# One of three fields of the sorted edges placed by GpSimd instead of VectorE

## The chip, the cores and the metric

The kernel runs on 1 core of one Trainium2 chip. The metric is the device time of one execution in microseconds (us), lower is better; a version's time is the median of its runs.

## What is computed

The reference is four message-passing layers over one graph: 3125 nodes with 128 features, 103125 directed edges. Each layer normalizes the node features, gathers them along the edges, and sums or softmax-averages messages at the edges' targets:

```python
edge_index = jnp.stack([src, dst])
h = jnp.maximum(_layernorm(x, axis=-1), 0.0)
x = x + _L0_gnn_ref(h, edge_index, edge_attr_32, edge_type_2, edge_weight, ...)
h = jnp.maximum(_layernorm(x, axis=-1), 0.0)
x = x + _L1_gnn_ref(h, L1_gnn_W1, L1_gnn_w2, src, dst)
h = jnp.maximum(_layernorm(x, axis=-1), 0.0)
x = x + _L2_gnn_ref(h, edge_index, edge_attr_2, ...)
h = jnp.maximum(_layernorm(x, axis=-1), 0.0)
x = x + _L3_gnn_ref(h, edge_index, edge_type_16, ...)
```

The change is in none of the layers but in what prepares the last three of them: the edges are sorted by the block of 128 nodes in which their source lies, so that a layer can work on dense blocks.

## The kernel before, in words

After layer 0 the kernel sorts the edges once. The nodes form NB = 25 blocks of 128. All edges whose target lies in block b make bucket b; a bucket is read as a window of 128 x 36 edges (EPP = 36 edges in each of 128 partitions) and is spread over KT = 50 tiles of 128 edges, two for each source block. An edge has three fields to carry along: a packed word (edge type, source and target within their blocks) and two attributes.

The five engines run the sort as a pipeline over the buckets, each with its own loop in program order, and semaphores between them. Per bucket:

- **SyncE** (`sp_sort`) loads the window `edge_in` into a ring of RING_E = 4 buffers and stores the finished bucket's rows.
- **VectorE, classes** (`dve_classes`, L2850, L2853) marks which of the 25 source blocks each edge belongs to, and counts.
- **VectorE, route** (`dve_route`, L2858 to L2878) gives each edge a slot: a scan and a reduce (L2860 to L2862), then tile number `tile_i` and position `pos_i`. L2874 writes `minus_pos`, which ScalarE waits for. L2875 writes the mask `in_tile` (128 x 36 x 50: edge is in tile k), and L2878 multiplies it by the three fields into `routed_v` (128 x 36 x 3 x 50), the multiply that is changed.
- **ScalarE** (`act_sort`) turns the positions into one-hot columns `hot_pos`: 36 instructions of L2957, then L2960 over all of them.
- **TensorE** (`pe_sort`, L2994) multiplies, for each of the 36 edges of a partition, one-hot position by routed fields and adds up in PSUM. In the profile that is 72 matmuls a bucket, of 128x150.
- **VectorE, unpack** (`dve_unpack`, L2884 to L2903) takes the sums out of PSUM and splits the packed word by many operations on 128x50 integers, then the attributes into bf16 parts.
- **GpSimd** does nothing in this loop.

`hot_pos`, `routed_v` and `minus_pos` have two buffers, `edge_in` four; `in_tile` has one. VectorE's order is fixed by the loop of `dve_sort`:

```python
for n in range(NB + 2):
    if n < NB:
        dve_classes(e, own, n)
    if 0 <= n - 1 < NB:
        dve_route(e, own, n - 1)
    if n >= 2:
        dve_unpack(e, own, n - 2)
```

So after the multiply of bucket b comes the unpacking of bucket b-1, which waits for TensorE's sums of that bucket (`packed_pe`), then the classes of b+2 and the route of b+1. In the profile the tensors show by the arena they lie in: `in_tile`, `edge_in`, `member`, `rank`, `tile_i` in arena_b, `routed_v`, `unpack_i` in arena_a, `hot_pos` in arena_c. Later, in layers 1 to 3, GpSimd builds one-hot masks (L3119, L3411, L3129) and clears buffers (L3123) while VectorE works on other parts of the same layers.

Of the kernel before, what the change touches and what calls it, by code (L numbers as in the profile page):

```python
# [21 lines left out]
NB = -(-N // P)  # L22
# [60 lines left out]
def turns(k, ring):  # L83

    return k // ring + 1
# [218 lines left out]
class BucketSignals:  # L304


    def __init__(self, g):
        spare = iter(g.of_layer0() + g.of_runs())

        def pair():  # L310
            return [next(spare), next(spare)]


        self.own = next(spare)
        self.consts = next(spare)
        self.d_list = next(spare)
        self.listed = next(spare)
        self.d_table = next(spare)
        self.d_start = next(spare)
        self.start = next(spare)  # L320
        self.d_keys = g.d_begin_keys
        self.d_window = pair() + pair()
        self.tot_dve = next(spare)
        self.pre_pe = next(spare)
        self.pre_used = next(spare)
        self.routed = next(spare)
        self.weighed = next(spare)
        self.spread = next(spare)
        self.away = next(spare)
        self.packed_pe = next(spare)  # L330
        self.fields = next(spare)
        self.turned_pe = next(spare)
        self.rows_act = next(spare)
        self.d_rows = pair()
        self.flag = next(spare)

        self.d_logits = next(spare)
        self.spread_lo = next(spare)
        self.hot = next(spare)
        self.counted_pe = next(spare)  # L340
        self.counted_act = next(spare)
        self.maxed = next(spare)
        self.diag = next(spare)
        self.negmax_pe = next(spare)
        self.exps = next(spare)
        self.weights = next(spare)
        self.mean_pe = next(spare)
        self.mean_used = next(spare)

        self.d_small = next(spare)  # L350
        self.split_act = next(spare)
        self.split_dve = next(spare)
        self.wc_set = next(spare)
        self.d_wc = next(spare)
        self.d_unit = pair() + [self.d_table, self.d_logits]
        self.attr_zero = next(spare)
        self.row_hot = next(spare)
        self.h_pe = next(spare)
        self.squared = next(spare)
        self.terms_set = next(spare)  # L360
        self.summed = next(spare)

        self.d_counted = self.d_rows
        self.d_pair_count = self.d_window
        self.low = self.routed
        self.low3 = self.weighed
        self.col_hot_pool = self.spread
        self.col_hot3_pool = self.away
        self.drawn_pe = self.pre_pe
        self.drawn = self.tot_dve  # L370
        self.scaled = next(spare)
        self.relu = next(spare)
        self.col_hot = next(spare)
        self.added_pe = next(spare)
        self.block_dve = next(spare)
        self.extra_pe = next(spare)
        self.extra_dve = next(spare)

        self.types_set = next(spare)
        self.d_types = next(spare)  # L380
        self.d_unit3 = pair() + [self.d_start]
        self.d_chunk = self.d_list
        self.typed = self.consts
        self.types_zero = self.flag
        self.row_hot3 = next(spare)
        self.h3_pe = next(spare)
        self.relu3 = next(spare)
        self.col_hot3 = next(spare)
        self.added3_pe = next(spare)
        self.block3_dve = next(spare)  # L390


def program(nc, a, out):
    ctx = ExitStack()
    with ctx:
# [2367 lines left out]
        def sp_sort(e):  # L2763
            e.wait_ge(g.phase_ended, 4)
            for signal in g.of_layer0():
                cleared = e.sem_clear(signal)
            cleared.then_inc(g.phase_begun, 1)
            e.wait_ge(sig.listed, 1)
            sp_load_tiled(e, sig.d_list, raw_tiled[:, 0], a["src"], 1)
            sp_load_tiled(e, sig.d_list, raw_tiled[:, 1], a["dst"], 1)  # L2770
            sp_load_tiled(e, sig.d_list, raw_tiled[:, 2], a["edge_type_16"], 1)
            sp_load_tiled(e, sig.d_list, raw_attr, a["edge_attr_2"].rearrange("e k -> (e k)"), 2)
            e.dma_start(lasts, row_bc(first_last[1, :], NB)).then_inc(sig.d_start, 16)
            e.wait_ge(sig.start, 2)
            e.dma_start(start_row.rearrange("(b o) -> b o", o=1), begin_i[1], allow_slow_non_contiguous=True).then_inc(sig.d_start, 16)
            e.wait_ge(sig.d_start, 32)
            e.dma_start(begin_row_i, start_row.unsqueeze(0)).then_inc(sig.d_start, 16)
            e.wait_ge(sig.listed, 2)
            e.dma_start(edge_table.rearrange("(c p f) w -> p c (f w)", c=TC, p=P), edges.rearrange("p (c f) w -> p c (f w)", c=TC)).then_inc(sig.d_table, 16)
            e.wait_ge(sig.d_start, 48)  # L2780
            e.wait_ge(sig.d_table, 16)
            for n in range(NB + 3):
                for j in (0, 1, 2) if n == 0 else (n + 2,):
                    if j < NB:
                        s = j % RING_E
                        if j >= RING_E:
                            e.wait_ge(sig.weighed, j - RING_E + 1)
                        first = e.value_load(begin_row_i[0:1, j:j + 1], min_val=0, max_val=E)
                        e.dma_start(edge_in[s], edge_table[bass.ds(first, WINDOW), :].rearrange("(p j) w -> p j w", p=P)).then_inc(sig.d_window[s], 16)
                if n >= 3:  # L2790
                    sp_store_bucket(e, n - 3)
            e.wait_ge(sig.flag, 1)
# [62 lines left out]
        def dve_route(e, own, b):  # L2855
            s = b % 2
            e.wait_ge(sig.pre_pe, b + 1)
            own.step(e.tensor_tensor(member[s][:, :, 0], bank[s][:, 0:NB], class_base, ALU.add))  # L2858
            flat = lambda v: v.rearrange("p k j -> p (k j)")
            own.step(e.tensor_tensor_scan(flat(rank), flat(restart), flat(member[s]), 0.0, ALU.mult, ALU.add))  # L2860
            own.step(e.tensor_tensor(rank[:, :, 1:], rank[:, :, 1:], member[s][:, :, 1:], ALU.mult))
            own.mark(e.tensor_reduce(slot_f, rank[:, :, 1:].rearrange("p k j -> p j k"), AX, ALU.add))  # L2862
            if b < NB - 1:

                own.step(e.tensor_scalar(over_f, rank[:, b, 1:], (2.0 * b + 3) * P, (KT - 2 * b - 3.0) * P, ALU.is_ge, ALU.mult))
                own.step(e.tensor_tensor(slot_i, slot_f, over_f, ALU.add))
            else:
                own.settle()
                own.step(e.tensor_copy(slot_i, slot_f))
            own.mark(e.tensor_scalar(tile_i, slot_i, 7, None, ALU.arith_shift_right))  # L2870
            own.step(e.tensor_scalar(pos_i, slot_i, P - 1, None, ALU.bitwise_and))
            if b >= 2:
                e.wait_ge(sig.packed_pe, b - 1)
            e.tensor_scalar(minus_pos[s], pos_i, -1.0, None, ALU.mult).then_inc(sig.routed, 1)  # L2874
            own.step(e.tensor_tensor(in_tile, bc(tile_i, 2, KT), bc(tile_row, 1, EPP), ALU.is_equal))  # L2875
            if b == 0:
                e.wait_ge(sig.squared, 1)
            e.tensor_tensor(routed_v[s], bc(in_tile, 2, 3), bc(edge_in[b % RING_E][:, :, 1:4], 3, KT), ALU.mult).then_inc(sig.weighed, 1)  # L2878

        def dve_unpack(e, own, b):  # L2880
            s = b % 2
# [54 lines left out]
        def pool_sort(e):  # L2936
# [3 lines left out]
            e.iota(tile_row, [[1, KT]], base=1, channel_multiplier=0, allow_small_or_imprecise_dtypes=True).then_inc(sig.consts, 1)  # L2940
            e.wait_ge(sig.start, 1)
            pool_gather(e, first_of, dst_keys, begin_i[0], sig.d_keys)
            e.wait_ge(sig.flag, 1)

        def act_sort(e):
# [30 lines left out]
        def pe_sort(e):  # L2976
            pause(e)
            for n in range(NB + 2):
# [7 lines left out]
                if 0 <= n - 1 < NB:  # L2986
                    b = n - 1
                    s = b % 2
                    e.wait_ge(sig.spread, b + 1)
                    e.wait_ge(sig.weighed, b + 1)  # L2990
                    if b >= 2:
                        e.wait_ge(sig.fields, b - 1)
                    for j in range(EPP):
# [18 lines left out]
        def sp_buckets(e):  # L3012
# [43 lines left out]
                sp_unit3(e, u)  # L3056
            e.wait_ge(g.nodes_ready, 8)
            sp_feature_rows(e, ("L3_gnn_msg_b", "L3_gnn_upd_b", "L3_gnn_ln_g", "L3_gnn_ln_b"))
            e.wait_ge(sig.types_set, 1)
            for i in range(3):  # L3060
                e.dma_start(E48[NT16 * i:NT16 * (i + 1), :], em_parts[:, i, :]).then_inc(sig.d_types, 16)
            for u in range(RING_U, 2 * NB):
# [4 lines left out]

        def sp_wc(e):

            e.wait_ge(sig.wc_set, 1)  # L3070
            for row, (i, part) in enumerate(((0, 0), (0, 1), (0, 2), (1, 0), (1, 1), (1, 2), (0, 0), (0, 1), (1, 0), (1, 1), (0, 0), (1, 0))):
                e.dma_start(Wc12[row:row + 1, :], wc_parts[i:i + 1, part, :]).then_inc(sig.d_wc, 16)

# [781 lines left out]
```

## Time and profile before

| | before |
|---|---|
| median of 3 runs | 4701.85 us (4698.02 to 4704.81) |
| the profiled execution, its own time | 4679.63 us |
| its span in the profile | 4677.9 us |
| VectorE busy | 3316.0 us (71%) |
| TensorE busy, matmuls | 3381.6 us (72%) |
| ScalarE busy | 2085.2 us (45%) |
| GpSimd busy | 1899.9 us (41%) |

The profiled execution is 22 us shorter than the median of the runs, so a sum made on its rows is a difference, to be added to either time. "Busy" counts an instruction from its start to its end in the record; an instruction that has been issued but is held up inside its engine counts as busy too. Consecutive instructions of an engine overlap by up to some 0.1 us in the record. The sort's loop over buckets lies from 2081 to 2574 us of the span. Outside it the change touches only two waits of SyncE, by their counts.

### The profile page before, as it was taken

The page shows a single profiled execution, that of the slowest core. Times are in us where ns is not written, and L with a number is a line of the kernel's source. Part 1 is how long each engine was busy: PE and PEld are TensorE (multiplying, and loading weights), DVE is VectorE, ACT ScalarE, POOL GpSimd, SP SyncE. Part 2 cuts the span into 40 slices and gives each one's busy share as a digit, 9 for nine tenths or more (in the row PEclk, how much of TensorE's full clock was granted, in tenths as well). Part 3 has the DMA queues.
Part 4 walks back from the last instruction along what each step waited for, and adds up shares of the span by engine and source line. Part 5 has one row for each costly group of instructions (what it writes and reads, how often), then busy time and mean ns, then how long its engine had stood idle before and what let it go on. Part 6 is the DMA issues. An engine that isn't in the chain of part 4 may idle for free.

```text
span 4677.9 us, 86004 instructions
## 1 busy us (share of the span) xinstructions
PE 3381.6 (72%) x31039; PEld 2815.7 (60%) x31039; DVE 3316.0 (71%) x6623; ACT 2085.2 (45%) x6143; POOL 1899.9 (41%) x2178
## 2 busy tenths in 40 slices
PE   1477777777777776326666467885789999969996
PEld 1255544454555554216666367784489999859995
DVE  5476666665666665459998688786766666679997
ACT  2344444444545553228787356673022222224443
POOL 0355566665666664100000130000045555538884
PEclk7677777776777776667777688997899999979998
DMA  4655555564555553010000121102344444313332
GB/s 108 187 156 155 154 160 154 155 153 142 166 159 167 158 167 103 16 38 8 12 12 9 56 79 60 43 38 90 117 122 125 126 126 126 107 53 127 128 129 70
DMA packets 368019, 498.45 MB, mean 107 GB/s; under 512 B 76530, under 2 KB 307636, under 8 KB 367453
## 3 DMA queue, kind: packets, MB, share of 16 engines
q1 hardware_dynamic: 313437, 328.51, 23.1%
q0 software_dynamic: 54144, 164.25, 12.6%
q8 instruction: 256, 4.19, 0.4%
q14 instruction: 182, 1.49, 0.1%
HBM read 381.76 MB, written 110.84 MB: 105 GB/s over the span
## 4 chain that ended last, share of the span: by engine, by line
PE 40%; DVE 22%; ACT 14%; issue 10%; another core or an unknown queue 5%; POOL 4%; DMA 3%; SPq 2%; ACTq 0%; DVEq 0%; POOLq 0%
PE psum L3691 4%; PE psum L3707 3%; PE psum L3642 3%; PE psum L3640 3%; PE psum L2490 3%; POOL arena_a L1172 3%; ACT arena_a L1366 3%; PE psum L2994 3%; ACT arena_c L2957 3%; PE psum L3607 2%; DVE arena_a L3187 2%; PE psum L3666 2%; PE psum L2425 2%; PE psum L3689 2%
## 5 line engine op out<-in xcount | busy, mean ns | idle before, releaser
L1172 POOL DMA_INDIRECT arena_a<-src_table,src_tix x808 | 820.8, 1016 | 430.1 <-issue 385.2
L3411 POOL TENSOR_SCALAR node_hot<-arena_c 128x128 fp32r<-128x128 f32 x575 | 368.7, 652 | 901.8 <-DVE arena_c L3299 568.6
L3429 DVE SCALAR_TENSOR_TENSOR msg_parts<-psum,msg_parts 128x512 fp32r<-128x512 f32 (+2 forms) x644 | 425.3, 660 | 259.9 <-ACT msg_parts L3578 227.8
L3129 POOL TENSOR_SCALAR node_hot_dst<-arena_c 128x128 fp32r<-128x128 f32 x587 | 383.9, 671 | 122.4 <-DVE arena_c L3533 67.9
L3578 ACT ACTIVATE msg_parts<-psum 128x512 fp32r<-128x512 f32 (+2 forms) x325 | 186.4, 574 | 520.4 <-PE psum L3642 520.4
L2994 PE MATMUL psum<-arena_a,arena_c 128*128 128x150 f32 x1800 | 289.4, 331 | 173.3 <-ACT arena_c L2960 173.3
L3640 PE MATMUL psum<-arena_c,arena_a 128*128 128x128 bf16 x3675 | 406.4, 220 | 0.0
L3642 PE MATMUL psum<-arena_c,arena_a 128*128 128x128 bf16 x3675 | 406.4, 220 | 0.0
L2994 PEld LDWEIGHTS psum<-arena_a,arena_c 128*128 128x128 f32 x1800 | 283.8, 225 | 176.4 <-ACT arena_c L2960 176.4
L1366 ACT ACTIVATE arena_a<-arena_a 128x128 f32<-128x128 f32 x808 | 238.5, 300 | 338.6 <-issue 259.2
L2433 PE MATMUL psum<-win_parts,pick_w 128*128 128x256 f32 x1616 | 381.4, 387 | 0.1
L2433 PEld LDWEIGHTS psum<-win_parts,pick_w 128*128 128x128 f32 x1616 | 274.5, 231 | 149.8 <-issue 148.8
L2408 PE MATMUL psum<-arena_b,win_w 3*128 3x512 bf16 x202 | 93.1, 461 | 357.3 <-ACT pick_w L1383 299.5
L3119 POOL TENSOR_SCALAR arena_a<-arena_a,arena_c 128x2500 bf16<-128x2500 bf16 x8 | 63.5, 7937 | 705.5 <-DMA arena_a<-bucket_lists 705.5
L1352 ACT ACTIVATE arena_c<-psum 128x272 f32<-128x272 f32 x404 | 161.0, 399 | 413.1 <-remote 323.2
L3638 PE MATMUL psum<-src_tix,arena_a 128*128 128x128 bf16 x1225 | 272.4, 222 | 70.9 <-DVE arena_a L3315 37.2
L2425 PE MATMUL psum<-weights,arena_c 128*128 128x512 f32 x404 | 318.8, 882 | 0.0
L1853 DVE TENSOR_TENSOR arena_a<-arena_a,psum 128x512 f32<-128x512 f32 x202 | 138.7, 687 | 251.9 <-remote 184.1
L1210 POOL TENSOR_TENSOR arena_c<-arena_c,weights 128x8 f32<-128x8 f32 x101 | 171.4, 1697 | 357.1 <-ACT arena_a L1366 354.2
L3691 PE MATMUL psum<-arena_c,arena_a 128*128 128x128 bf16 x3675 | 308.9, 219 | 0.0
L2957 ACT ACTIVATE arena_c<-arena_c,arena_b 128x128 f32<-128x128 f32 x900 | 265.8, 387 | 90.1 <-DVE arena_b L2874 90.1
L3593 ACT ACTIVATE msg_parts<-psum 128x512 fp32r<-128x512 f32 (+1 forms) x319 | 185.4, 581 | 260.4 <-PE psum L3691 260.4
(581 smaller groups left out, 10177.8 us busy)
## 6 DMA issues: line engine op xcount, KB each, us to landing
y_rows<-arena_c SPq DMA_DIRECT2D x101, 576.0 KB
arena_a<-bucket_rows SPq DMA_DIRECT2D x150, 384.0 KB
arena_a<-bucket_rows SPq DMA_DIRECT2D x50, 448.0 KB
arena_a<-bucket_lists SPq DMA_DIRECT2D x25, 896.0 KB
pair_counts<-arena_c SPq DMA_DIRECT2D x25, 800.0 KB
arena_a<-bucket_lists SPq DMA_DIRECT2D x25, 704.0 KB
arena_a<-src_table,src_tix POOLq DMA_INDIRECT x808
arena_c<-edge_attr SPq DMA_DIRECT2D x101, 128.0 KB
```

Source lines behind the costliest of these rows:

```text
L1172: e.indirect_dma_start(out_, None, table, bass.IndirectOffsetOnAxis(ap=idx, axis=0)).then_inc(sem, 16)
L1366: sq = e.activation(GS[r][:, t, 2 * D:3 * D], GS[r][:, t, 2 * D:3 * D], ACT.Square, accum_out=d2[:, t:t + 1])
L2425: e.matmul(bank[0][:, :], eat[k % RING_EA][:, hf, :], Wt4[:, :], start=True, stop=True).then_inc(g.addend_pe, 1)
L2433: rows = e.matmul(picked[:, t, :], pick_w[s][:, 4 * hf + t, :], win_parts[s][:, part, :], start=(part == 0), stop=(part == 1))
L2957: away = e.activation(hot_pos[s][:, j, :], iota_row, ACT.Abs, bias=minus_pos[s][:, j:j + 1])
L2994: put = e.matmul(bank[2 + s][:, 0:3 * KT], hot_pos[s][:, j, :], routed_v[s][:, j, :, :].rearrange("p f k -> p (f k)"), start=(j == 0), sto ...
L3129: return e.tensor_scalar(node_hot3[at % RING_H][:, i, :], iota_row, dst_lo[:, b, t:t + 1], None, ALU.is_equal)
L3411: return e.tensor_scalar(node_hot[at % RING_M][:, i, :], iota_row, src_lo[:, b, 2 * k + j:2 * k + j + 1], None, ALU.is_equal)
L3429: e.scalar_tensor_tensor(out=to[:, 1, 0:nt, :], in0=bank[at % 4][:, 0:nt * P].rearrange("p (t f) -> p t f", f=P), scalar=0.0, in1=to[:, 0, ...
L3640: e.matmul(to, row_hot[0][s][:, c_], A3[:, part, sb_ * D:(sb_ + 1) * D], start=False, stop=False)
L3642: put = e.matmul(to, row_hot[1][s][:, c_], B3[:, part, b * D:(b + 1) * D], start=False, stop=(part == 2))
L3691: put = e.matmul(to, src_rows3[s][:, c_], A3[:, part, k * D:(k + 1) * D], start=False, stop=(part == 2))
```

## The change

The multiply that places the fields is split. VectorE still makes the mask and multiplies it by two of the fields (the packed word and the first attribute), 128 x 3600 elements in place of 128 x 5400. GpSimd gets a loop of its own over the 25 buckets in `pool_sort`: for each it waits for the window, for the mask and for the free buffer of `routed_v`, and multiplies the mask by the second attribute, 128 x 1800 elements. Both read the same mask, and both wait for the same count of the new semaphore `tiled`, which the mask's instruction raises. VectorE writes the next mask only when GpSimd has done with this one (`weighed_pool`, b), TensorE starts its matmuls only when both parts are there, and SyncE refills a window's buffer only when both have read it. `tiled` and `weighed_pool` share semaphores with `types_set` and `wc_set`, whose waits now start from NB = 25.

```diff
--- before.py
+++ after.py
@@ -347,6 +347,7 @@
         self.mean_pe = next(spare)
         self.mean_used = next(spare)
 
+        self.types_set = next(spare)
         self.d_small = next(spare)
         self.split_act = next(spare)
         self.split_dve = next(spare)
@@ -360,6 +361,8 @@
         self.terms_set = next(spare)
         self.summed = next(spare)
 
+        self.tiled = self.types_set
+        self.weighed_pool = self.wc_set
         self.d_counted = self.d_rows
         self.d_pair_count = self.d_window
         self.low = self.routed
@@ -376,7 +379,6 @@
         self.extra_pe = next(spare)
         self.extra_dve = next(spare)
 
-        self.types_set = next(spare)
         self.d_types = next(spare)
         self.d_unit3 = pair() + [self.d_start]
         self.d_chunk = self.d_list
@@ -2785,6 +2787,7 @@
                         s = j % RING_E
                         if j >= RING_E:
                             e.wait_ge(sig.weighed, j - RING_E + 1)
+                            e.wait_ge(sig.weighed_pool, j - RING_E + 1)
                         first = e.value_load(begin_row_i[0:1, j:j + 1], min_val=0, max_val=E)
                         e.dma_start(edge_in[s], edge_table[bass.ds(first, WINDOW), :].rearrange("(p j) w -> p j w", p=P)).then_inc(sig.d_window[s], 16)
                 if n >= 3:
@@ -2872,10 +2875,13 @@
             if b >= 2:
                 e.wait_ge(sig.packed_pe, b - 1)
             e.tensor_scalar(minus_pos[s], pos_i, -1.0, None, ALU.mult).then_inc(sig.routed, 1)
-            own.step(e.tensor_tensor(in_tile, bc(tile_i, 2, KT), bc(tile_row, 1, EPP), ALU.is_equal))
+            if b:
+                e.wait_ge(sig.weighed_pool, b)
+            e.tensor_tensor(in_tile, bc(tile_i, 2, KT), bc(tile_row, 1, EPP), ALU.is_equal).then_inc(sig.tiled, 1)
             if b == 0:
                 e.wait_ge(sig.squared, 1)
-            e.tensor_tensor(routed_v[s], bc(in_tile, 2, 3), bc(edge_in[b % RING_E][:, :, 1:4], 3, KT), ALU.mult).then_inc(sig.weighed, 1)
+            e.wait_ge(sig.tiled, b + 1)
+            e.tensor_tensor(routed_v[s][:, :, 0:2, :], bc(in_tile, 2, 2), bc(edge_in[b % RING_E][:, :, 1:3], 3, KT), ALU.mult).then_inc(sig.weighed, 1)
 
         def dve_unpack(e, own, b):
             s = b % 2
@@ -2940,6 +2946,14 @@
             e.iota(tile_row, [[1, KT]], base=1, channel_multiplier=0, allow_small_or_imprecise_dtypes=True).then_inc(sig.consts, 1)
             e.wait_ge(sig.start, 1)
             pool_gather(e, first_of, dst_keys, begin_i[0], sig.d_keys)
+
+            e.wait_ge(sig.squared, 1)
+            for b in range(NB):
+                e.wait_ge(sig.d_window[b % RING_E], 16 * turns(b, RING_E))
+                e.wait_ge(sig.tiled, b + 1)
+                if b >= 2:
+                    e.wait_ge(sig.packed_pe, b - 1)
+                e.tensor_tensor(routed_v[b % 2][:, :, 2, :], in_tile, bc(edge_in[b % RING_E][:, :, 3], 2, KT), ALU.mult).then_inc(sig.weighed_pool, 1)
             e.wait_ge(sig.flag, 1)
 
         def act_sort(e):
@@ -2988,6 +3002,7 @@
                     s = b % 2
                     e.wait_ge(sig.spread, b + 1)
                     e.wait_ge(sig.weighed, b + 1)
+                    e.wait_ge(sig.weighed_pool, b + 1)
                     if b >= 2:
                         e.wait_ge(sig.fields, b - 1)
                     for j in range(EPP):
@@ -3056,7 +3071,7 @@
                 sp_unit3(e, u)
             e.wait_ge(g.nodes_ready, 8)
             sp_feature_rows(e, ("L3_gnn_msg_b", "L3_gnn_upd_b", "L3_gnn_ln_g", "L3_gnn_ln_b"))
-            e.wait_ge(sig.types_set, 1)
+            e.wait_ge(sig.types_set, NB + 1)
             for i in range(3):
                 e.dma_start(E48[NT16 * i:NT16 * (i + 1), :], em_parts[:, i, :]).then_inc(sig.d_types, 16)
             for u in range(RING_U, 2 * NB):
@@ -3067,7 +3082,7 @@
 
         def sp_wc(e):
 
-            e.wait_ge(sig.wc_set, 1)
+            e.wait_ge(sig.wc_set, NB + 1)
             for row, (i, part) in enumerate(((0, 0), (0, 1), (0, 2), (1, 0), (1, 1), (1, 2), (0, 0), (0, 1), (1, 0), (1, 1), (0, 0), (1, 0))):
                 e.dma_start(Wc12[row:row + 1, :], wc_parts[i:i + 1, part, :]).then_inc(sig.d_wc, 16)
 
```

## Rows read from the trace of the kernel before

**Rows 1.** Chain that ended last, two buckets: start us, us, engine, tile, line, count

```profile
2149.34 10.64 ACT arena_c L2957 x36
2160.00 4.05 ACT arena_c L2960
...
2164.10 12.50 PE psum L2994 x72
2176.62 0.22 DVE arena_a L2884
...
2187.77 7.42 ACT arena_c L2957 x25
```

**Rows 2.** Timeline of VectorE, one bucket: start us, us, engine, line, op, out<-in

```profile
2130.37 0.18 DVE L2874 TENSOR_SCALAR arena_b<-arena_b 128x36 f32<-128x36 int32 x1
2130.47 2.03 DVE L2875 TENSOR_TENSOR arena_b<-arena_b,arena_a 128x1800 f32<-128x1800 int32 x1
2132.53 5.78 DVE L2878 TENSOR_TENSOR arena_a<-arena_b 128x5400 f32<-128x5400 f32 x1
2138.23 0.20 DVE L2884 CAST arena_a<-psum 128x50 int32<-128x50 f32 x1
2138.47 0.19 DVE L2885 TENSOR_SCALAR arena_a<-arena_a 128x50 int32<-128x50 int32 x1
...
2140.29 0.26 DVE L2903 TENSOR_TENSOR weights<-arena_a,weights 128x100 bf16<-128x100 f32 x1
2140.47 1.77 DVE L2850 TENSOR_TENSOR arena_b<-arena_b,arena_c 128x900 f32<-128x900 f32 x1
...
2149.12 0.18 DVE L2874 TENSOR_SCALAR arena_b<-arena_b 128x36 f32<-128x36 int32 x1
```

**Rows 3.** The line L2874 by its source: durations in ns min/median/max, first and last start

```profile
L2874 DVE TENSOR_SCALAR arena_b<-arena_b x25: 182/183/185, 2092.8 to 2543.8; 128x36 f32<-128x36 int32 x25
```

**Rows 4.** Busy time from the first L2874 to the last, by engine

```profile
2092.80:2543.80 451.00, 287.31 (x1862) 280.41 (x1863) 435.38 (x632) 367.85 (x956) 0.00 (x0) 0.77 0.05 10
```

**Rows 5.** Timeline of TensorE, one odd and one even bucket; in brackets the idle time before

```profile
2315.90 11.69 PE L2994 MATMUL psum<-arena_a,arena_c 128*128 128x150 f32 x72 [7.13 <-ACT arena_c L2960]
2334.64 10.88 PE L2994 MATMUL psum<-arena_a,arena_c 128*128 128x150 f32 x72 [6.18 <-ACT arena_c L2960]
```

**Rows 6.** Timeline of GpSimd, then of VectorE, around one L3119 in layer 1

```profile
2801.08 7.39 POOL L3119 TENSOR_SCALAR arena_a<-arena_a,arena_c 128x2500 bf16<-128x2500 bf16 x1 [20.82 <-DMA arena_a<-bucket_lists]
...
2801.41 0.68 DVE L3180 SCALAR_TENSOR_TENSOR arena_c<-arena_c 128x512 f32<-128x512 f32 x1
2802.01 6.23 DVE L3187 CUSTOM_DVE_ANT_0 arena_a<-arena_b,arena_a 128x512 f32<-128x512 f32 x1
...
2809.41 0.69 DVE L3187 CUSTOM_DVE_ANT_0 arena_a<-arena_b,arena_a 128x512 f32<-128x512 f32 x1
```

**Rows 7.** Timeline of VectorE, then of GpSimd, around the clearing L3123

```profile
4101.72 0.47 DVE L3411 TENSOR_SCALAR node_hot<-arena_c 128x128 fp32r<-128x128 f32 x2
...
4104.10 2.26 DVE L3411 TENSOR_SCALAR node_hot<-arena_c 128x128 fp32r<-128x128 f32 x2
...
4103.13 6.25 POOL L3123 MEMSET arena_a<- 128x3584 bf16 x2 [0.47 <-PE psum L3642]
```

**Rows 8.** Timeline of VectorE and of GpSimd, then GpSimd's line L3129 by its source

```profile
4303.84 1.15 DVE L3489 TENSOR_SCALAR arena_a<-arena_a,node_id 128x3584 bf16<-128x3584 bf16 x1
...
4304.23 1.22 POOL L3129 TENSOR_SCALAR node_hot_dst<-arena_c 128x128 fp32r<-128x128 f32 x1 [1.68 <-PE psum L3707]
...
L3129 POOL TENSOR_SCALAR node_hot_dst<-arena_c x587: 596/603/1443, 4180.3 to 4617.4; 128x128 fp32r<-128x128 f32 x196
```

**Rows 9.** Integer and float operations of VectorE by their source, as in rows 3

```profile
L2825 DVE TENSOR_SCALAR arena_c<-arena_a x1: 607/607/607, 2061.2 to 2061.2; 128x896 int32<-128x896 int32 x1
...
L2853 DVE TENSOR_REDUCE arena_b<-arena_b x25: 1090/1092/1093, 2083.2 to 2520.9; 128x25 f32<-128x900 f32 x25
```

**Rows 10.** GpSimd's clearing line by form: count, busy us, mean ns

```profile
L3123 POOL MEMSET arena_a<- 128x3584 bf16 x2 | 6.3, 3158 | 0.5 <-PE psum L3642 0.5
```

## The prediction

> **What bounds the kernel now.** I read the page first: the loop of the sort is 490 us of a span of 4678, and GpSimd idles in it. Then the chain of waits, to see which engine ends last there. It goes round: ScalarE from 2149.34, 10.64 + 4.05 us, then TensorE, 12.50 us, then VectorE from L2884 until the next L2874, then ScalarE again at 2187.77 [rows 1]. That round serves one bucket, and two rounds are under way at a time (odd and even buckets), so it takes 38.43 us for two buckets, 19.2 for one. Then VectorE's timeline over one bucket: from L2874 to L2874 it is 2149.12 - 2130.37 = 18.75 us without a gap [rows 2]. So two limits lie almost on each other: VectorE's own work of 18.75 a bucket, and the round of 18.7 to 19.2. All 25 buckets confirm it: first to last L2874 is 2543.8 - 2092.8 = 451.0 us for 24 steps, 18.79 each [rows 3], with VectorE busy for 435.4 us of it and GpSimd for none [rows 4]. The round varies with TensorE's part: 11.69 for an odd bucket, 10.88 for the even one behind it [rows 5].
>
> All times below count from T, the end of a bucket's L2874 (2130.55 in rows 2).
>
> **The change, part by part.**
>
> *VectorE's multiply gets shorter.* L2875 and L2878 have 1800 and 5400 elements and take 2.03 and 5.78 us [rows 2]: 3.75 us for 3600 elements, 1.04 ns each. With 3600 elements the multiply takes 5.78 - 1.88 = 3.90 us. It starts at T+1.98 and ends at T+5.88, where it ended at T+7.76. That alone gives little, since the round does not contain the multiply: ScalarE has started at T, and TensorE waits for ScalarE until T+14.8, long after the fields are there. VectorE would only wait for TensorE instead of working: its step would be 16.87 us, the round's 18.75. Even buckets, held up now by VectorE's order, could follow TensorE's shorter time [rows 5]: mean of 11.69 and 10.88 in place of 11.69 is 0.4 us per two buckets, at most 5 us in all.
>
> *GpSimd's multiply is added, and it shares something with VectorE.* Both multiplies start on the same count. What happens when the two engines meet is in layer 1 [rows 6]: while L3119 runs on GpSimd, VectorE's L3187 takes 6.23 us, and 0.69 us when alone. It was held for 5.54 us. GpSimd's instruction itself had begun 0.93 us before it got its way, at a boundary between two instructions of VectorE, and ended at 2808.47, 0.92 us after VectorE was let go (2808.24 - 0.69 = 2807.55). All eight L3119 have such a partner. So one excludes the other for whole instructions. By the Trainium skill ("SBUF — State Buffer", section "Who interferes with whom"), a VectorE instruction with two SBUF inputs, or one in a two-port mode, and a GpSimd instruction that reads SBUF block each other completely, the one that starts first going first; by that rule the trace agrees, with 6.23 against 0.69 us.
>
> *Which of the two goes first?* VectorE starts L2878 0.03 us after the mask [rows 2]; GpSimd has waits in front of it and needed up to 0.93 us from its start [rows 6]. I take VectorE first. GpSimd then gets in at T+5.88.
>
> *How long does it hold VectorE?* No row has this multiply. The nearest is L3119, a long GpSimd instruction that reads and writes a tile: 5.54 us for 2500 elements is 2.22 ns each, 3.99 us for 1800, and 0.92 us from there to its end. Bounds: below, the clearing, which reads nothing, with 3.16 us for 3584 elements [rows 10], 0.88 ns each, 1.6 us for 1800; above, the 128-element mask with 0.60 us [rows 8], 4.7 ns each, 8.5 us. By the skill's "GPSIMD Engine Reference", section "Performance versus the Vector engine", a two-input operation on 2048 fp32 elements takes 4497 ns, 3.95 us for 1800 if scaled (an estimate); with a hold of 3.6 the sum below would be +31 us instead.
>
> *What is held?* Behind the multiply stands the unpacking of the bucket before: L2884 reads PSUM, and from L2885 on come small operations on integers in SBUF, one input each. Do these wait too? Two rows say so. Two L3411 of VectorE, one input each, take 2.26 us during the clearing on GpSimd and 0.47 together before it [rows 7]; they end at 4106.36, so they were let go at 4105.9, about 0.3 us before the first of the two clearings ends (4103.13 + 3.16 [rows 10], less the overlap of the two). And GpSimd's L3129 takes 1.22 us during L3489 and 0.60 otherwise [rows 8]. The integer operations of the sort are of that fast kind: L2825 takes 0.607 us for 896 elements, where a reduce of 900 takes 1.09 [rows 9]. So L2885 waits for GpSimd, until somewhere between the end of its reads (3.99) and 0.3 before its end (3.99 + 0.92 - 0.3 = 4.6). I take 4.3.
>
> *The sum.* GpSimd holds from T+5.88 to T+10.18. From L2885 (2138.47) to the next T (2149.30) VectorE needs 10.83 us [rows 2]. The new step is 5.88 + 4.3 + 10.83 = 21.0 us against 18.79. The round is no longer the limit: TensorE's sums are there at 26.8 - 21.0 = T+5.8. The first and the last of the 24 steps lack a part: the first has no unpacking, about 18.6 (the blocked instruction is L2850, let go with the reads), the last has no classes (1.77 and 1.09 us), about 18.1. Sum: 22 x 21.0 + 18.6 + 18.1 = 498.7 us, against 451.0: **47.7 us more**. TensorE's wait for GpSimd's part is hidden: GpSimd ends at T+5.88+4.91 = T+10.8, TensorE starts at T+14.8. If GpSimd needed 4 us more, that cover would be gone. VectorE's next mask waits for GpSimd until T+10.8 and comes at T+21: hidden. SyncE's refill waits for a bucket three back: hidden. The profiled execution would go from 4679.6 to 4727.3; the median of the runs, 22 us higher, from 4701.85 to **4749.5**.
>
> **The rivals.**
>
> 1. *The small operations pass.* Then GpSimd's 3.99 us fall into VectorE's own idle time. VectorE waits for TensorE until T+8.0 anyway, then unpacks; the first operation with two SBUF inputs is L2903, 2.06 us later, at T+10.1, and GpSimd has read all by T+9.9. The step stays at the round: between 18.6 and 18.8, from 4697 to 4702, no slower. For it: 50 elements are few, and no row shows an operation that short being held. Against: rows 7 and 8. The same result comes if GpSimd is quicker than I think: the loss is gone when the hold is below 18.79 - 5.88 - 10.83 = 2.1 us, near the lower bound. Chance 0.19, 0.04 of it for a gain over 9 us.
> 2. *GpSimd goes first.* Then L2878 waits 4.0 us, ends at T+10.2, and L2884 to T follows with 11.07: a step of 21.2, 52 us more, 4754. For it: both wait for the same count. Against: the waits in front of GpSimd and its late start [rows 6]. Chance 0.10.
> 3. *GpSimd is slow.* With 8.5 us the hold makes a step of 25.2, about 150 us more, 4850, and TensorE begins to wait for it too. It speaks for it that short instructions cost that rate; against, that L3119 does not. Chance 0.05.
>
> The forecast has the rest, 0.66. That the change does less than it says cannot be: GpSimd has 25 new instructions and VectorE's multiply has a third less.
>
> **How the numbers follow.** A measurement of this kernel can tell about 0.2%, 9.4 us, from no change. The forecast's own range: a hold of 3.0 us gives +18 us, 4.9 gives +61, 5.4 gives +73. I give 4716 to 4775, which leaves out rival 1 and rival 3, and takes in rival 2. Faster by over 0.2%: 0.04. Within: 0.15 (rival 1). Slower: 0.81.
>
> **What would show it.** Right: one small operation behind L2884 recorded with some 4 us, in nearly every bucket; VectorE's multiply at 3.9 us; GpSimd's multiply recorded longer than its work (it waits 3.9 us for VectorE), some 8 us; a step of 21 us; no wait of L2884 for TensorE. Wrong in the kind: all small operations at 0.18 to 0.19 us and VectorE idle for 2 us before L2884, with the step at 18.7. Rival 2 would show a multiply of VectorE of 8 us and GpSimd's one of 5. The size is wrong if GpSimd's hold is not near 4.3 us.

## The result, and the profile after

| | before | changed |
|---|---|---|
| median of 5 runs | 4698.02 us (4693.24 to 4704.81) | 4717.76 us (4711.72 to 4722.67) |
| ratio | | 1.0045, 95% interval 1.0032 to 1.0058 |
| span of the profiled execution | 4677.9 us | 4718.2 us |

By the medians the change costs 19.7 us, 0.42%; the ratio, taken over all runs, is 0.45%. That is slower by more than the 9.4 us that the prediction allowed for a measurement, and on the forecast side, but it is less than half of the 47.7 us that were forecast. The two profiled executions differ by 40 us, and half of that is no effect of the change: the sort's first `minus_pos` starts at 2114.2 us of the span where it was 2092.8 [rows 3], before anything has changed; in another profile of the same changed kernel (below) it starts at 2084.9. So the sort's loop is read by itself, from the first `minus_pos` to the last.

In the changed kernel's lines `minus_pos` is L2877, the mask L2880, VectorE's multiply L2884, GpSimd's multiply L2956, the unpacking L2890 to L2909, the classes L2853 and L2856. The lines by their source, durations in ns min/median/max, first and last start, which answer to [rows 3]:

```profile
L2877 DVE TENSOR_SCALAR arena_b<-arena_b x25: 183/184/185, 2114.2 to 2582.2; 128x36 f32<-128x36 int32 x25
L2884 DVE TENSOR_TENSOR arena_a<-arena_b x25: 3908/3908/3911, 2116.5 to 2584.4; 128x3600 f32<-128x3600 f32 x25
L2891 DVE TENSOR_SCALAR arena_a<-arena_a x25: 191/1831/2755, 2140.4 to 2609.9; 128x50 int32<-128x50 int32 x25
L2956 POOL TENSOR_TENSOR arena_a<-arena_b x25: 6905/6913/6932, 2116.5 to 2584.5; 128x1800 f32<-128x1800 f32 x25
```

The loop takes 2582.2 - 2114.2 = 468.0 us in place of 451.0: 17.0 us more, nearly all of the 20. VectorE's multiply is at 3.91 us as worked out. L2891, an operation on 128x50 integers, was 0.19 us long in every bucket and is now 1.83 us in the median. GpSimd's multiply is recorded with 6.91 us, more than half of them spent waiting. One bucket in the timelines of VectorE and then of GpSimd (start us, us, engine, line, op, out<-in, in brackets the idle time before):

```profile
2171.33 0.18 DVE L2877 TENSOR_SCALAR arena_b<-arena_b 128x36 f32<-128x36 int32 x1
2173.49 3.91 DVE L2884 TENSOR_TENSOR arena_a<-arena_b 128x3600 f32<-128x3600 f32 x1
2177.66 0.21 DVE L2890 CAST arena_a<-psum 128x50 int32<-128x50 f32 x1 [0.26 <-PE psum L3009]
2177.90 2.64 DVE L2891 TENSOR_SCALAR arena_a<-arena_a 128x50 int32<-128x50 int32 x1
...
2191.02 0.18 DVE L2877 TENSOR_SCALAR arena_b<-arena_b 128x36 f32<-128x36 int32 x1
...
2173.59 6.91 POOL L2956 TENSOR_TENSOR arena_a<-arena_b 128x1800 f32<-128x1800 f32 x1 [12.80 <-DVE arena_b L2880]
```

Where the time goes can be read off. Both multiplies start at once, VectorE's 0.1 us ahead. GpSimd's must wait until VectorE's is done (2173.49 + 3.91 = 2177.40), then runs for some 3.1 us, to 2180.50. L2890 reads PSUM and passes; L2891 has to wait until 2180.35 (2177.90 + 2.64 - 0.19). From there to the next `minus_pos` it is the same work as before. The step is 2191.02 - 2171.33 = 19.69 us. The hold is seen undiluted in the first bucket, where the classes' compare stands right behind the multiply:

```profile
2120.29 4.73 DVE L2853 TENSOR_TENSOR arena_b<-arena_b,arena_c 128x900 f32<-128x900 f32 x1
```

It takes 1.77 us otherwise [rows 2], so the hold is 2.96 us, 1.64 ns for each of 1800 elements. In the later buckets VectorE first spends a part of that time waiting for TensorE's sums (0.15 to 2.2 us before L2890), and L2891 shows only the rest.

### The profile page after: what moved, and what is told of

Its sections match the earlier page's. It is cut to its first block, busy times and chain, and to the rows that moved or that the text cites. A ratio compares the mean times of both kernels' runs of the same rounds, so it can differ in the third digit from the quotient of the medians.

```text
span 4718.2 us, 86098 instructions
## 1 busy us (share of the span) xinstructions
PE 3380.3 (72%) x31039; PEld 2817.1 (60%) x31039; DVE 3311.3 (70%) x6623; ACT 2082.3 (44%) x6143; POOL 2064.0 (44%) x2203
## 4 chain that ended last, share of the span: by engine, by line
PE 38%; DVE 21%; ACT 15%; issue 11%; another core or an unknown queue 7%; POOL 4%; SPq 2%; DMA 2%; ACTq 0%; DVEq 0%; POOLq 0%
PE psum L3706 4%; PE psum L3722 3%; PE psum L3657 3%; PE psum L3655 3%; POOL arena_a L1174 3%; PE psum L3009 3%; ACT arena_a L1368 3%; PE psum L2492 3%; ACT arena_c L2971 3%; PE psum L3622 2%; PE psum L3681 2%; DVE arena_a L3202 2%; PE psum L3294 2%; PE psum L3704 2%
## 5 line engine op out<-in xcount | busy, mean ns | idle before, releaser
L2956 POOL TENSOR_TENSOR arena_a<-arena_b 128x1800 f32<-128x1800 f32 x25 | 172.8, 6914 | 333.5 <-DVE arena_b L2880 333.5
```

## The experiments

Theory A is that of the prediction: the multiply on GpSimd keeps out VectorE's operations with two SBUF inputs, or of the fast kind of [rows 9], for a whole instruction. Theory B is its rival: the waits that the change adds between the engines cost the time. "Loop" is always from the first `minus_pos` to the last. All runs of one job are on one chip, with runs of the kernel before; chips and jobs differ (4671 to 4698 us for before, in one job 4387), so ratios are taken within a job. The kernel before has one profile, so every loop is set beside its 451.0 us, also where it is of another chip; the changed kernel's loop was the same on two chips (468.0 and 467.8 us, below).

### GpSimd's work taken away

```diff
-                e.tensor_tensor(routed_v[b % 2][:, :, 2, :], in_tile, bc(edge_in[b % RING_E][:, :, 3], 2, KT), ALU.mult).then_inc(sig.weighed_pool, 1)
+                if b < 2:
+                    e.memset(routed_v[b][:, :, 2, :], 0.0).then_inc(sig.weighed_pool, 1)
+                else:
+                    e.drain().then_inc(sig.weighed_pool, 1)
```

> The third field is cleared once for both buffers and never filled; GpSimd keeps its waits and its signals for every bucket but does no work from the third on. Theory A (GpSimd's multiply keeps VectorE out for about 3 us a bucket): no small operation is held, the step goes from 19.70 to the round of 18.6 to 18.8 us, first to last minus_pos 446 to 451 us in place of 468.0, total within 5 us of before. Theory B (the added waits between the engines cost it, not the work): step stays at 19.7, total stays 17 to 20 us over before.

Ratio to before 0.9991 (0.9981 to 1.0002). Loop 2540.7 - 2093.5 = 447.2 us. L2891 is never longer than 192 ns:

```profile
L2877 DVE TENSOR_SCALAR arena_b<-arena_b x25: 183/184/185, 2093.5 to 2540.7; 128x36 f32<-128x36 int32 x25
L2891 DVE TENSOR_SCALAR arena_a<-arena_a x25: 191/191/192, 2120.2 to 2567.3; 128x50 int32<-128x50 int32 x25
```

All waits of the change are still there, and the loss is gone, so theory B falls. And a third of VectorE's multiply saved brings 451.0 - 447.2 = 3.8 us: with VectorE's work in this order, that is all the change could have won had GpSimd been free of cost.

### The small operations moved out of SBUF

```diff
-        unpack_i = [words(A_, 12065 + i * KT, [P, KT], I32) for i in range(3)]
+        unpack_i = [bank[7][:, 64 + i * 64:64 + i * 64 + KT].bitcast(I32) for i in range(3)]
```

(and TensorE's totals of both parities in bank 6, to free bank 7).

> GpSimd's multiply as in the changed kernel; the integers of the unpacking lie in PSUM instead of SBUF, so that its small operations read and write PSUM. Theory A with the hold at L2891 (an operation on SBUF in a two-port mode): nothing is held before the cast of the attributes some 1.8 us later; step 18.7 to 18.9, loop 448 to 453 us, total within 5 us of before. Theory B, or a hold that does not depend on where the operands lie: step 19.7, loop 468.

Ratio to before 0.9992 (0.9977 to 1.0006), loop 2546.8 - 2099.2 = 447.6 us, with GpSimd's multiply at work as before:

```profile
L2877 DVE TENSOR_SCALAR arena_b<-arena_b x25: 183/184/185, 2099.2 to 2546.8; 128x36 f32<-128x36 int32 x25
L2891 DVE TENSOR_SCALAR psum<-psum x25: 218/218/218, 2125.8 to 2573.2; 128x50 int32<-128x50 int32 x25
L2908 DVE CAST weights<-arena_a x10: 211/473/966, 2127.6 to 2295.4; 128x100 bf16<-128x100 f32 x10
L2956 POOL TENSOR_TENSOR arena_a<-arena_b x25: 6906/6913/6935, 2101.5 to 2549.0; 128x1800 f32<-128x1800 f32 x25
```

The operation that was held for 1.6 us in the median is not held at all when its operands are in PSUM (0.218 us, always). The next operation that goes from SBUF to SBUF, the cast L2908 some 1.8 us later, takes the rest of the hold in some buckets, 0.97 us in place of 0.21. This shows rival 1 of the prediction as a kernel of its own: what made the difference was where the operands lie.

### GpSimd's share doubled

```diff
-            e.tensor_tensor(routed_v[s][:, :, 0:2, :], bc(in_tile, 2, 2), bc(edge_in[b % RING_E][:, :, 1:3], 3, KT), ALU.mult).then_inc(sig.weighed, 1)
+            e.tensor_tensor(routed_v[s][:, :, 0, :], in_tile, bc(edge_in[b % RING_E][:, :, 1], 2, KT), ALU.mult).then_inc(sig.weighed, 1)
```

(and GpSimd multiplies fields 1 and 2.)

> GpSimd multiplies two fields (3600 elements), VectorE one (1800). Theory A: VectorE's multiply takes 2.03 us and ends at 4.0 us behind minus_pos, GpSimd then keeps it out for twice 2.96, 5.9 us, until 9.9; with 10.8 us of VectorE's work behind, a step of 20.7 us and a loop of about 495 us. If the hold has a fixed part of 1 us: 8.9, 19.7, 470. Theory B: GpSimd ends before TensorE starts in any case, so step 19.7, loop 468.

One run: 4730.35 us, before 4679.35 in the same job. Loop 2594.8 - 2099.4 = 495.4 us, as expected to half a microsecond. VectorE's timeline, then GpSimd's:

```profile
2162.08 2.03 DVE L2884 TENSOR_TENSOR arena_a<-arena_b 128x1800 f32<-128x1800 f32 x1
2166.17 0.21 DVE L2890 CAST arena_a<-psum 128x50 int32<-128x50 f32 x1 [2.05 <-PE psum L3009]
2166.41 3.86 DVE L2891 TENSOR_SCALAR arena_a<-arena_a 128x50 int32<-128x50 int32 x1
...
2162.18 8.04 POOL L2956 TENSOR_TENSOR arena_a<-arena_b 128x3600 f32<-128x3600 f32 x1 [12.81 <-DVE arena_b L2880]
```

L2891 is let go at 2166.41 + 3.86 - 0.19 = 2170.08, 5.97 us behind the end of VectorE's multiply (2164.11): 1.66 ns an element, with no fixed part to speak of.

### GpSimd writes and does not read

The multiply becomes `e.memset(routed_v[b % 2][:, :, 2, :], 0.0)` in every bucket.

> GpSimd clears the third field in every bucket (1800 elements written, nothing read) where it multiplied. Theory A, by which a two-input multiply of VectorE keeps out only what reads: GpSimd's clearing runs beside the multiply, about 1.6 us recorded, and has ended before L2891: step 18.6 to 18.8, loop 446 to 451. If the multiply keeps out writes too: GpSimd recorded with 5 to 6 us, VectorE held by up to 1.6 us from 5.9 on, still ending at 7.5, no loss either; the recorded length tells the two apart. Theory B: 468.

One run: 4677.96 us against 4679.35. Loop 2545.8 - 2096.8 = 449.0 us. The timelines of VectorE and GpSimd:

```profile
2154.04 3.91 DVE L2884 TENSOR_TENSOR arena_a<-arena_b 128x3600 f32<-128x3600 f32 x1
...
2154.11 1.61 POOL L2956 MEMSET arena_a<- 128x1800 f32 x1 [15.27 <-DVE arena_b L2880]
```

Clearing 1800 elements takes 1.61 us in full beside VectorE's multiply, which stays at 3.91: the same VectorE multiply that kept out GpSimd's multiply does not keep out a clearing, which reads nothing. The Trainium skill ("SBUF — State Buffer", section "Who interferes with whom") says that such an instruction contends with a GpSimd instruction that reads SBUF and not with one that only writes it; the trace agrees, with 1.61 and 3.91 us side by side. (The third field is left out of the result here: it is zeros.)

### The price of the form

In place of the multiply, GpSimd does what L3119 does, on memory that nothing else uses:

```diff
+                e.tensor_scalar(probe, probe, iota_col, None, ALU.is_equal).then_inc(sig.weighed_pool, 1)
```

`probe` is 128x2500 in bf16 in the one kernel, in fp32 in the other. The third field is cleared once in both, and so left out of the sums.

> In place of the multiply GpSimd does in every bucket what L3119 does in layer 1: compare 128x2500 bf16 in place with a scalar per partition, on memory that nothing else uses (the third field is cleared and left out). If the form of the instruction sets the price: VectorE held for 5.54 us from 5.9 us behind minus_pos on, step 5.9 + 5.5 + 10.8 = 22.2 us, loop about 530 us. If every GpSimd instruction in this place has the multiply's 1.64 ns an element: 4.1 us, step 20.8, loop about 500.

> The same compare on 2500 fp32 elements. If the scalar compare is what is slow, the hold is 5.5 us as with bf16 (step 22.2, loop 530); if bf16 is, it is that of the multiply, 2500 x 1.64 ns = 4.1 us (step 20.8, loop 500) or less, since it has one input where the multiply has two.

4764.51 and 4761.94 us, before 4670.91. Loops 2629.6 - 2085.2 = 544.4 us and 2627.1 - 2082.6 = 544.5. GpSimd and VectorE in the bf16 kernel, one bucket:

```profile
2198.18 10.24 POOL L2962 TENSOR_SCALAR Hn<-Hn,node_id 128x2500 bf16<-128x2500 bf16 x1 [12.73 <-DVE arena_b L2881]
...
2198.06 3.91 DVE L2885 TENSOR_TENSOR arena_a<-arena_b 128x3600 f32<-128x3600 f32 x1
2201.88 0.20 DVE L2891 CAST arena_a<-psum 128x50 int32<-128x50 f32 x1
2202.12 6.34 DVE L2892 TENSOR_SCALAR arena_a<-arena_a 128x50 int32<-128x50 int32 x1
2207.61 0.89 DVE L2893 TENSOR_SCALAR arena_a<-arena_a 128x50 int32<-128x50 int32 x1
```

From the end of the multiply (2201.97) the compare runs to 2208.42: 6.45 us for 2500 elements, 2.6 ns each, in either type. The multiply took 3.1 us for 1800, 1.7 each. So it is the form of the instruction, not the type, that makes the price. Which part of the form does it, the compare, the scalar for each partition or the writing in place, no run tells apart. L3119 itself fits: 7.39 us recorded less 0.93 of waiting is 6.46 [rows 6]. L2892 was let go at 2208.27, 0.15 us before GpSimd's end; the pair of [rows 6] had a two-input operation let go 0.92 us before it. So the loop is 14 us above my 530: I had set 5.54 us for the hold, and for a scalar operation from SBUF to SBUF it is 6.3. The multiply of the changed kernel lets both kinds go 0.15 to 0.2 us before its end.

The first bucket of the bf16 kernel has a two-input operation beside the compare, the scan L2864, which takes 2.08 us otherwise. GpSimd's timeline, then VectorE's:

```profile
2089.02 10.30 POOL L2962 TENSOR_SCALAR Hn<-Hn,node_id 128x2500 bf16<-128x2500 bf16 x1
...
2087.38 3.91 DVE L2885 TENSOR_TENSOR arena_a<-arena_b 128x3600 f32<-128x3600 f32 x1
2091.21 1.76 DVE L2854 TENSOR_TENSOR arena_b<-arena_b,arena_c 128x900 f32<-128x900 f32 x1
...
2094.23 6.25 DVE L2864 TENSOR_TENSOR_SCAN arena_b<-arena_b 128x925 f32<-128x925 f32 x1
```

The scan is let go at 2094.23 + 6.25 - 2.08 = 2098.40, 0.92 us before the compare's end at 2099.32, as in [rows 6]. The same rows show that a waiting GpSimd does not always come next: its compare is recorded from 2.3 us before the end of VectorE's multiply (2091.29), yet the classes' compare L2854, with two inputs in SBUF, took its usual 1.76 us first. Counted back 6.45 us from its end, GpSimd's compare had its turn at 2092.87, about when L2854 ended. Why it came second here, and GpSimd's multiply first in the changed kernel, stays open.

### The changed kernel once more

> The changed kernel once more, for a closer interval: the loop 17 us longer than before (468.0 against 451.0), so the ratio 1.0036 to 1.0045 if nothing outside the loop changes with it; 1.002 or 1.006 would mean that other stages move too.

Ratio 1.0035 (1.0023 to 1.0048), loop 2552.7 - 2084.9 = 467.8 us. The loop's 17 us are 0.36% of 4680 us; no other stage needs to have changed.

### Both limits moved: the classes first

The prediction said that VectorE's work and the round through ScalarE and TensorE limit together, so that neither alone is worth anything. To test it, the classes of bucket b+2 are put ahead of the unpacking of bucket b, into VectorE's wait for TensorE:

```diff
+            dve_classes(e, own, 0)
             for n in range(NB + 2):
-                if n < NB:
-                    dve_classes(e, own, n)
                 if 0 <= n - 1 < NB:
                     dve_route(e, own, n - 1)
+                if n + 1 < NB:
+                    dve_classes(e, own, n + 1)
                 if n >= 2:
                     dve_unpack(e, own, n - 2)
```

The job of these runs has 4387 us for the kernel before, and no profile of it. First on the kernel before:

> The kernel before, with the classes of bucket b+2 ahead of the unpacking of bucket b in VectorE's order, so that they lie in its wait for TensorE and no longer in the round. Two limits (VectorE's own work 18.75 us, the round 18.7): the round falls to 17.3, VectorE's work stays: step 18.75, first to last minus_pos 449 to 451 us, total unchanged within 3 us. If the round alone were the limit before: step 17.3, total 35 us less.

Ratio 0.9987 (0.9978 to 0.9996), loop 2247.4 - 1802.3 = 445.1 us: 6 us less, and 5.8 us less by the medians, more than the 3 us that I had allowed. Of these, 2.3 us I had not seen: the second step of before was 21.1 us long, since the first bucket's sums come late, and is 18.8 now. But it is far from the 35 us that a single limit would have given.

Then with two fields and no work on GpSimd:

> Two fields on VectorE, none on GpSimd (the third field is cleared once and left out), and the classes first. Both limits fall: VectorE's work to 16.87 us, the round to 17.2 to 17.35 (14.8 of ScalarE, 11.3 to 11.7 of TensorE, 8.2 of VectorE, for two buckets). Step about 17.3, loop 410 to 416 us, total 33 to 38 us below before. If something else limits (the windows' loads, ScalarE with 15.5 us), the step is longer and the row before minus_pos shows its wait.

Ratio 0.9907 (0.9892 to 0.9922), loop 2206.7 - 1795.7 = 411.0 us. Less work alone gave 3.8 us, the order alone 5.9, both together 40.0. That is the two limits.

With the multiply really done by GpSimd, the order alone does not do:

> The changed kernel with the classes first, nothing else. Theory A: the classes' first operation has two inputs in SBUF and stands right behind the multiply, so it is held for 2.96 us in every bucket and VectorE's work becomes 16.87 + 2.96 = 19.8 us: step 19.8, loop about 473, total 20 to 25 us over before. If GpSimd's multiply could be hidden by order alone: step 17.3.

One run: 4406.21 us against 4387.2; loop 2268.5 - 1797.4 = 471.1 us. The compare of the classes is now what stands behind the multiply:

```profile
L2853 DVE TENSOR_TENSOR arena_b<-arena_b,arena_c x25: 1735/4733/4751, 1786.0 to 2237.9; 128x900 f32<-128x900 f32 x25
```

It is held for 2.96 us in nearly every bucket. The last kernel gives it its second input from PSUM (25 class numbers, and the bucket's offset as a constant):

```diff
-            own.step(e.tensor_tensor(member[s][:, :, 1:], bc(edge_in[b % RING_E][:, :, 0], 1, NB), bc(class_rows[:, b, :], 2, EPP), ALU.is_equal))
+            own.step(e.scalar_tensor_tensor(out=member[s][:, :, 1:], in0=bc(edge_in[b % RING_E][:, :, 0], 1, NB), scalar=-32.0 * b, in1=bc(class_ps, 2, EPP), op0=ALU.add, op1=ALU.is_equal))
```

> The whole work: GpSimd's multiply, the classes first, and the class numbers (the second input of the classes' compare) read from PSUM, so that the compare has one input in SBUF; the totals of TensorE share one bank to free one. Theory A: compare and reduce of the classes run beside GpSimd's 2.96 us, the unpacking comes when it has ended; VectorE's work 16.9, the round 17.3: step 17.3 to 17.5, loop 412 to 420 us, total 30 to 36 us below before, no operation of VectorE held. If one input in SBUF is held as well: step 19.8 as without PSUM.

Ratio to before **0.9914** (0.9900 to 0.9928): 4349.36 us against 4387.2 on the same chip, 38 us less. Loop 2216.0 - 1803.7 = 412.3 us, 1.3 more than without any work on GpSimd; the total fell by 2 us more than the 36 expected. The timelines of VectorE and GpSimd:

```profile
1996.31 3.91 DVE L2886 TENSOR_TENSOR arena_a<-arena_b 128x3600 f32<-128x3600 f32 x1
2000.13 1.83 DVE L2855 SCALAR_TENSOR_TENSOR arena_b<-arena_b,psum 128x900 f32<-128x900 f32 x1
2002.00 1.09 DVE L2858 TENSOR_REDUCE arena_b<-arena_b 128x25 f32<-128x900 f32 x1
2003.18 0.21 DVE L2892 CAST arena_a<-psum 128x50 int32<-128x50 f32 x1
2003.43 0.19 DVE L2893 TENSOR_SCALAR arena_a<-arena_a 128x50 int32<-128x50 int32 x1
...
1996.41 6.92 POOL L2959 TENSOR_TENSOR arena_a<-arena_b 128x1800 f32<-128x1800 f32 x1 [10.14 <-DVE arena_b L2882]
```

GpSimd's multiply runs from about 2000.2 to 2003.33. Beside it lie the compare (one input in SBUF, one in PSUM), the reduce (one input) and the cast from PSUM, none of them held; L2893, which would be, starts 0.1 us after GpSimd has ended. This kernel beats the kernel before, with all three fields computed, and the kernel before in the new order too, by 32 us (4381.45). The new order by itself is not what won.

## Why the prediction was right in kind and wrong in size

- **What bounds the kernel**: held. Two limits at 18.75 and 18.7 to 19.2 us; less work alone 3.8 us, as worked out ("at most 5 us"), both together 40.
- **VectorE's multiply at 3.90 us**: 3.91.
- **Which goes first**: VectorE, in all 25 buckets, as taken; rival 2 did not come.
- **What is held**: L2891, as taken from [rows 7 to 9], in 23 of its 25 buckets; for the last two, TensorE's sums come only when GpSimd's last multiply has ended. Shown by moving its operands to PSUM. Rival 1, by which the small operations pass, did not come: it takes operands in PSUM.
- **The working of the sum**: 5.88 + hold + 10.83. With the measured hold of 3.0 it gives 19.7 us a step; measured 19.69. The loop's 22 full steps are 19.7 each, the first 17.7, the last 16.8, together 468.0. Two figures beside the sum were slightly off: for a hold of 3.0 us the sum's own terms give +17 and not +18, and rival 2, with GpSimd's 4.0 us first, gives T+9.9 and some 47 us, not T+10.2 and 52.
- **The step that failed** is "How long does it hold VectorE?". I took 4.3 us from L3119, the nearest row by length and by having a tile for its input. It was 3.0. L3119 is a compare with a scalar per partition, and that form costs 2.6 ns an element against 1.7 for the multiply, in bf16 and in fp32. The 1.3 us too much, 24 times, are the 31 us between 47.7 and 17.0. The estimate from the Trainium skill's figure ("GPSIMD Engine Reference", section "Performance versus the Vector engine"), +31 us, was nearer, and still too high: 3.95 us for GpSimd's multiply, where the trace has about 3.1, and a hold of 2.96. The measurement decides.
- **The signs**: "one small operation with some 4 us" was 0.7 to 2.75 us, and "no wait of L2884 for TensorE" did not come true: the same operation, L2890 in the changed kernel, waits for TensorE in every bucket. Both follow from the shorter hold. With a step of 19.7 the sums are there at 26.8 - 19.7 = T+7.1, after the multiply's end at T+5.88 and before the hold's end at T+8.84; the wait lies inside the hold and costs nothing.
- **The range**: its lower end, 4716, was 14 us above before, and the measured 4717.76 lies 1.8 us inside it; but a hold of 3.0 us stood in it as an edge case, though the rows gave no reason to trust a compare's price for a multiply. The rows' bounds for the form were 0.88 and 4.7 ns; a middle of 2.2 was a choice, not a reading.
- **The other covers**: TensorE's start and VectorE's next mask did not wait for GpSimd, as said. SyncE's refill did, in two buckets (35.3 us in all), as it had waited twice for VectorE's multiply before (33.1 us); no engine had to wait for a window in the loop. With all these waits in place and no work, the loop was 447.2 us.

## What to carry to other kernels

Before work is given to an idle GpSimd, list what VectorE does next to it by where the operands lie: beside an instruction of GpSimd that reads SBUF, operations with two inputs in SBUF and copies or scalar operations from SBUF to SBUF stopped here for nearly all of its work; reduces and those with a PSUM operand ran on. Order them so that the second kind lies beside GpSimd, or put a small operand into PSUM; here that turned a loss of 0.4% into a gain of 0.9%. And price GpSimd by an instruction of the same form, not by the nearest length; a recorded duration there contains the waiting.

## What was not expected of the hardware

- On GpSimd a multiply of two tensors is cheaper for each element (1.64 to 1.66 ns of hold, for 1800 and for 3600 elements) than a compare of one tensor with a scalar per partition (2.6 ns from its turn to its end, bf16 and fp32 alike).
- When GpSimd runs that compare, a two-input operation of VectorE is let go 0.92 us before its recorded end [rows 6], a small scalar operation from SBUF to SBUF only 0.15 us before. The scan of the price kernels has the same 0.92 us. Why the two kinds differ stays open. It would fit if the reading were given back before the writing: the next operation, L2893, is recorded from 2207.61, 0.81 us before the compare's end, though L2892 ended only at 2208.46. No run tested that reason, and with GpSimd's multiply both kinds are let go about 0.2 us before its end, which it would have to explain as well.
